# x copied into the result ahead of time, and the last product added to it by accumulating transfers from GpSimd

## What is computed

```python
xn = layernorm(x)
s  = attention(xn, ...)          # differential attention, RMS norm per head, then @ Wo
g  = silu(ffn(xn, ...))          # two layers of a mixture of 6 experts (top 2) with 2 shared ones;
                                 # each layer ends with y * rsqrt(mean(y*y) + eps) * norm_w[j]
return x + s * g
```

## Time and profile before

| | |
|---|---|
| median of 3 runs | 2025.4 us (2024.9 to 2025.41) |
| profiled execution, its own time | 2026.82 us |
| its span, first to last instruction | 2024.8 us |
| TensorE busy, share of the span | 93% |
| mean granted TensorE clock | 0.967 of full speed |
| layer two's blocks | about 1727 to 1946 us |
| last stage | about 1946 us to the end |

### The profile page before, as it was taken

The page is one execution under the profiler, slowest core; times in us unless marked ns, Lnnn a source line. Parts: engine busy times, 40 slices in busy tenths (PEclk is TensorE's granted clock), DMA queues, the critical chain, the costliest instruction groups (busy, mean ns, idle before and its releaser), DMA issues. The chain is left out here.

```text
span 2024.8 us, 42105 instructions
## 1 busy us (share of the span) xinstructions
PE 1881.6 (93%) x11851; PEld 1121.7 (55%) x11851; DVE 1466.7 (72%) x3474; ACT 1050.6 (52%) x2538; POOL 676.0 (33%) x728
## 2 busy tenths in 40 slices
PE   7888999999999999999999999999899999999975
PEld 4543334444343443434444347777788888787864
DVE  7888888888888898888888844444468855333348
ACT  3324667676676666667666644444333322344444
POOL 4542432111111232322323214777603432233334
PEclk9976999999999999999999999999999999999988
DMA  4443332212222121211212103343312112244363
GB/s 126 142 129 100 108 106 77 66 29 70 57 63 83 41 62 41 61 49 50 61 41 62 40 12 93 120 128 123 116 42 99 71 51 67 86 128 128 97 234 107
DMA packets 196441, 170.43 MB, mean 84 GB/s; under 512 B 92105, under 2 KB 176377, under 8 KB 195961
## 3 DMA queue, kind: packets, MB, share of 16 engines
q1 hardware_dynamic: 177288, 119.95, 20.7%
q0 software_dynamic: 15888, 46.16, 6.5%
q10 hardware_dynamic: 3168, 3.15, 0.5%
HBM read 104.16 MB, written 72.70 MB: 87 GB/s over the span
## 5 line engine op out<-in xcount | busy, mean ns | idle before, releaser
L1772 DVE TENSOR_REDUCE mx<-ps 128x1 f32<-128x512 f32 (+3 forms) x1536 | 762.2, 548 | 107.8 <-PE ps L904 84.7
L1363 ACT ACTIVATE fbuf<-ps 128x512 f32<-128x512 f32 (+3 forms) x1024 | 459.2, 508 | 253.9 <-PE ps L915 241.6
L900 PE MATMUL ps<-rbuf 72*128 72x512 bf16 (+3 forms) x1536 | 506.7, 337 | 33.0 <-DVE mx L1772 21.4
L915 PE MATMUL ps<-rbuf 75*128 75x512 bf16 (+3 forms) x1536 | 500.5, 333 | 18.0 <-DMA rbuf<-mrows 16.0
L915 PEld LDWEIGHTS ps<-rbuf 75*128 75x128 bf16 x1536 | 150.4, 98 | 326.1 <-ACT fbuf L1363 143.2
L1363 ACT ACTIVATE gbuf<-ps 128x512 f32<-128x512 f32 (+2 forms) x512 | 210.4, 470 | 106.3 <-PE ps L915 86.7
L749 POOL TENSOR_SCALAR_AFFINE_SELECT gbuf<-gbuf 128x512 f32<-128x512 f32 x96 | 61.3, 638 | 532.5 <-ACT gbuf L1363 532.5
L900 PEld LDWEIGHTS ps<-rbuf 72*128 72x128 bf16 x1536 | 152.0, 99 | 147.3 <-DVE mx L1772 101.2
L930 PE MATMUL ps<-fbuf 128*32 128x512 f32 (+3 forms) x2048 | 230.1, 522 | 3.1 <-ACT fbuf L1352 1.1
L904 PE MATMUL ps<-maskq,identb 128*128 128x128 bf16 x1024 | 230.3, 225 | 0.0
L756 POOL DMA_INDIRECT y_scr<-wstage,bidx x138 | 137.8, 998 | 248.1 <-ACT wstage L1407 222.2
(11 more groups left out here) (273 smaller groups left out, 2990.8 us busy)
## 6 DMA issues: line engine op xcount, KB each, us to landing
rbuf<-q_scr SPq DMA_DIRECT2D x192, 96.0 KB
xs_scr<-in_pad SPq DMA_DIRECT2D x8, 1360.0 KB, 6.2
gbuf<-xs_scr SPq DMA_DIRECT2D x69, 136.0 KB
gbuf<-xe_scr SPq DMA_DIRECT2D x69, 136.0 KB
rbuf<-k_scr SPq DMA_DIRECT2D x192, 48.0 KB
gbuf<-y_scr SPq DMA_DIRECT2D x8, 1024.0 KB
q_scr<-gbuf SPq DMA_DIRECT2D x48, 128.0 KB
gbuf<-a_scr SPq DMA_DIRECT2D x12, 512.0 KB, 5.0
```

What stands on the lines that cost most here:

```text
L900: ins = pe.matmul(o, qst[par][0:PROWS, i // 4, m, P * (i % 4):P * (i % 4 + 1)], kst[par][0:PROWS, m % 2, 512 * piece:512 * piece + width], ...
L915: pe.matmul(o, kst[par][0:SROWS, m % 2, P * j:P * (j + 1)], qst[par][0:SROWS, h, m, t0:C], start=True, stop=True).then_inc(b_scores, 1)
L1363: act.activation(prob(s)[:, t0:C], ps[:, s % SRING, t0:C], ACT.Exp, scale=SCALE).then_inc(b_exp, 1)
L1772: dve.tensor_reduce(mx[:, i // 4, piece, n:n + 1], ps[:, SRING + s % SRING, 0:width], AX, ALU.max, negate=True).then_inc(b_maxed, 1)
```

## The change

x no longer passes through SBUF in the last stage. Eight transfers of 512 KB from DRAM to DRAM copy x into the result; SP issues them after the row loads of blocks q = 10, 14, ..., 38. The product `gT` is then added to the result in DRAM by a transfer issued by GpSimd (`accum_op=ALU.add`), one for each chunk, the last one too. weigh(c) now waits until the transfer of chunk c - 2 has landed. GpSimd's additions, VectorE's last addition, the eight loads of x and SP's stores are gone. SP waits for all copies before it waits for the scatters of y and reloads it.

```diff
-            def load_x(c):
-                sp.dma_start(xres[c], xr[c]).then_inc(d_xearly if c < XEARLY else d_xlate, 16)
+            def copy_x(c):
+                sp.dma_start(ov[c], xr[c]).then_inc(d_xcopied, 16)
...
                 if odd == 0 and 0 <= i < NCH:
                     load_attn(i)
-                elif odd == 0 and NCH <= i < NCH + XEARLY:
-                    load_x(i - NCH)
-
-            sp.wait_ge(e_turned, TURNS)
-            sp.wait_ge(e_idx, TURNS)
-            load_x(3)
-            sp.wait_ge(e_u, TURNS)
-            load_x(4)
-            sp.wait_ge(e_down, TURNS)
-            load_x(5)
+                elif odd == 2 and 0 <= i < NCH:
+                    copy_x(i)
+
+            sp.wait_ge(d_xcopied, 16 * NCH)
             sent(1)
             for c in range(YSLOTS):
                 load_last_y(c)
-            load_x(6)
-            sp.wait_ge(d_turned, 3)
-            load_x(7)
             for c in range(YSLOTS, NCH):
                 load_last_y(c)
-            for c in range(NCH):
-                if c < NCH - 1:
-                    sp.wait_ge(d_fin, c + 1)
-                else:
-                    sp.wait_ge(d_sg, NCH + 1)
-                sp.dma_start(ov[c], xw[:, TB * c:TB * (c + 1), 0:E]).then_inc(d_out[c % 2], 16)
...
             def finish(c):
+
+                pool.wait_ge(d_xcopied, 16 * NCH)
                 pool.wait_ge(d_sg, c + 1)
-                if c < XEARLY:
-                    pool.wait_ge(d_xearly, 16 * XEARLY)
-                else:
-                    pool.wait_ge(d_xlate, 16 * (NCH - XEARLY))
-                pool.tensor_tensor(xw[:, TB * c:TB * (c + 1), 0:E], gT[:, c % 2].rearrange("p (k n) -> p k n", k=TB),
-                                   xres[c], ALU.add).then_inc(d_fin, 1)
+                pool.dma_start(ov[c], gT[:, c % 2].rearrange("p (k n) -> p k n", k=TB), accum_op=ALU.add
+                               ).then_inc(d_out[c % 2], 16)
 
             for c in range(NCH):
                 inv_rms(NCH + c)
                 if c > 0:
                     finish(c - 1)
+            finish(NCH - 1)
...
                 if c < 2:
                     dve.wait_ge(d_turned, c + 1)
                 else:
-                    dve.wait_ge(d_fin, c - 1)
+                    dve.wait_ge(d_out[c % 2], 16 * (c // 2))
...
-            dve.wait_ge(d_sg, NCH)
-            dve.wait_ge(d_xlate, 16 * (NCH - XEARLY))
-            dve.tensor_tensor(xw[:, NB - TB:NB, 0:E], gT[:, (NCH - 1) % 2].rearrange("p (k n) -> p k n", k=TB),
-                              xres[NCH - 1], ALU.add).then_inc(d_sg, 1)
```

More of the change, by code:

```diff
@@ L231, in build @@
         ain = [quarter(buf, i) for buf in (gbuf, rbuf[:, :].bitcast(F32)) for i in range(4)]
-        xres = [quarter(fbuf, 1), quarter(fbuf, 2), quarter(fbuf, 4), quarter(gbuf, 4), quarter(wqk, 0), quarter(fbuf, 3),
-                quarter(wstage[:, :, :].rearrange("p a n -> p (a n)"), 0), quarter(gbuf, 2)]
-        XEARLY = 3
         ytile = []
@@ L314, in build @@
         d_out = [sem(f"d_out{h}") for h in range(2)]
-        d_ain, d_xearly, d_xlate = sem("d_ain"), sem("d_xearly"), sem("d_xlate")
+        d_ain, d_xcopied = sem("d_ain"), sem("d_xcopied")
         d_yin = [sem(f"d_yin{s}") for s in range(YSLOTS)]
-        d_turned, d_aT, d_proj, d_nw, d_g, d_sg, d_fin = (
-            sem("d_turned"), sem("d_aT"), sem("d_proj"), sem("d_nw"), sem("d_g"), sem("d_sg"), sem("d_fin"))
+        d_turned, d_aT, d_proj, d_nw, d_g, d_sg = (
+            sem("d_turned"), sem("d_aT"), sem("d_proj"), sem("d_nw"), sem("d_g"), sem("d_sg"))
         block = ctx.enter_context(nc.Block())
@@ L804, in _ @@
                 send_out(1, q)
+            ov = out.rearrange("b (h k p) e -> (b h) p k e", h=2, p=P)
             def finish(c):
+                pool.wait_ge(d_xcopied, 16 * NCH)
                 pool.wait_ge(d_sg, c + 1)
-                if c < XEARLY:
-                    pool.wait_ge(d_xearly, 16 * XEARLY)
-                else:
-                    pool.wait_ge(d_xlate, 16 * (NCH - XEARLY))
-                pool.tensor_tensor(xw[:, TB * c:TB * (c + 1), 0:E], gT[:, c % 2].rearrange("p (k n) -> p k n", k=TB),
-                                   xres[c], ALU.add).then_inc(d_fin, 1)
+                pool.dma_start(ov[c], gT[:, c % 2].rearrange("p (k n) -> p k n", k=TB), accum_op=ALU.add
+                               ).then_inc(d_out[c % 2], 16)
             for c in range(NCH):
```

## The result

The changed kernel took 2038.48 us in the median of 8 runs, the kernel before 2024.67 us in the median of its 8. The ratio is 1.0076, with a 95% interval of 1.0059 to 1.0092: 0.8% slower, some 15 us. The forecast was 2031 us, slower, in a range of 2014 to 2048 us.

What follows compares the result with a forecast made beforehand. Bound: TensorE for most, VectorE in the last stage, slowed 2.1 us a turn by GpSimd's add. Copies +2.5, scatter -2.0, company +2.5, loop +2.2, last gate -1.2, end +1.7 = +5.7 us on 2025.4: 2031 us, range 2014 to 2048 us.

Steps and rivals of the forecast that it cites:

- L: Time from apply's end to its adding transfer's landing, taken as 5.75 us; the change's total is about 7 L - 34.6 us.
- the company: Last stage: the first adding transfer shares the DMA engines with the reload of y, +2.5 us (0 to +5).
- the late loads: Among the last four scatters: load_x(3) to (5) are gone, so the last scatter lands sooner, -2.0 us (0 to -2.5).
- the end: After apply(7): the last transfer's landing replaces VectorE's add of x and SP's store, +1.7 us (-0.6 to +3.9).
- the copies: Second layer's blocks: eight copies of x on SP's queue between row loads, +2.5 us (+1 to +7).
- the rival in which the addition was innocent: Last stage: GpSimd's add isn't what slows combine, VectorE's turn stays at 7.79 us; about +3 us, chance 0.04.
- The loop: Six turns from apply(0) to apply(6): each 8.15 us instead of 7.79 us, +2.2 us.
- Between apply(6) and apply(7): Last turn: squares and power are done early, so apply(7) ends 1.95 us after apply(6), not 3.15 us; -1.2 us.
- The quick: Last stage rival: the adding transfer lands in under 4.4 us; at 4.2 us the whole is -6 us; chance 0.20.
- the middling transfer: Last stage rival: the adding transfer lands in 4.4 to 5.5 us, no tellable change, 2021 to 2029 us; chance 0.18.
- the crowding copies: Blocks rival: copies hold up row loads at 1.08 us each, +7.1 us instead of +2.5 us, 2036 us; chance 0.08.
- The slow one: Last stage rival: adding serialises reading and writing row by row, landing in 8 us, +21 us, 2047 us; chance 0.18.

Runs made afterwards that it cites:

- e5: The kernel before, with GpSimd's seven additions of x moved to VectorE behind each apply; no copies, no adding transfers: 2013.95 us, ratio 0.9952.
- e10: The four-tile kernel of e1 with a GpSimd addition of gT to itself put ahead of each adding transfer: 2016.15 us, run once.
- e2: The changed kernel with GpSimd's transfers writing the product without adding, x left out of the result: 2020.31 us, run once.
- e1: The changed kernel with gT in four tiles instead of two, so weigh(c) waits for transfer c-4: 2013.81 us, ratio to before 0.996.
- e9: The changed kernel with gT in three tiles instead of two: 2011.75 us, ratio to before 0.9946.
- e7: The changed kernel with the reload of y left out for chunks 4 to 7: 2034.45 us, run once.
- e6: The four-tile kernel of e1 with the last chunk finished as before, VectorE adding x and SP storing: 2011.62 us, ratio to before 0.9941.
- e4: The kernel before with eight DRAM to DRAM copies of x into a scratch tensor added, its own loads of x kept: ratio 1.0005.
- e8: The changed kernel with the three late 512 KB loads of x put back, their data not used: 2039.02 us, run once.
- e3: The changed kernel with SP storing the product without adding, x left out of the result: 2017.59 us, run once.

## Why the prediction was right, point by point

The direction and the mechanism were as forecast: GpSimd's addition gone, VectorE's combines at 3.4 us, and in their place a wait of weigh for the landing. The size, +5.7 us against about +15 us by the ratio and +16.2 us in the traces, was too small, because L was mis-sized. The prediction names this as its own sign of failing: L outside 5.5 to 6.8 us. The direction held because L lies above the 4.9 us at which the forecast's line, 7 L - 34.6 us, is zero. With the measured L of 7.0 us that line gives +14.4 us. That it comes so close is in part luck, since the other misses nearly cancel: the company (+2.1 us), the late loads (+1.0 us) and the end (+0.8 us beyond the line) against the copies (-2.0 us).

- *What bounds the stage.* Right, and shown from both sides: e5 takes the addition away from GpSimd and the combines drop to 3.37 us; e10 puts one back and they rise to 5.01 us. This also removes the rival in which the addition was innocent.
- *L, 5.75 us.* This is the term that failed. The sum without the adding came out right, 0.1 + 2.05 + 1.45 + 0.7 = 4.3 us, where e2 measures 4.4 us on the mean. Its terms did not: the hand-over took 0.6 to 0.9 us, not 0.1 us, and from the start of the instruction to the landing it was mostly 3.4 us, where these terms give 4.2 us. The two errors cancel, which is luck. For reading the old values I took another pass at the full rate, 1.45 us. This is the step that failed: adding costs 2.6 us, by half the rate, a slow first microsecond, a tail, and 0.5 us more of descriptors. 7.0 - 5.75 = 1.25 us too little, paid seven times, are 8.8 us. The estimate of 4.4 us from the Trainium skill's two pages was lower still; the plain transfer of e2 takes as long.
- *The loop, +2.2 us.* Measured with the first turn's company set apart: 9.39 us a turn, 1.6 us over 7.79 us, times six, +9.6 us. e1 and e9 show that it is the wait: with three or four tiles, and no wait, a turn is 5.7 to 5.8 us, the 5.8 us that were worked out for VectorE alone.
- *The first transfer's company, +2.5 us.* Right in kind, too small: 14.01 - 9.39 = 4.6 us in the trace, 4.8 us by e7. It is the upper bound of 5 us.
- *Between apply(6) and apply(7), -1.2 us.* Measured -1.2 us.
- *The end, +1.7 us.* Measured +3.7 us. From the end of apply(7) to the landing it was 8.5 us, not 5.75 us, and the 4.5 us of closing, which I took as fixed, were 3.8 us. The last transfer is slower than the others (7.8 us from its start): apply(7) follows apply(6) by 1.93 us only, and transfer 6 started 1.7 us late, so the two start 0.95 us apart and share the engines. GB/s in 40 slices of 2020 to 2036 us has them in one stretch, the last byte at about 2031.6 us, 8.3 us after the end of apply(7):

```profile
GB/s 0 0 0 0 0 0 20 0 0 0 0 0 36 49 136 159 189 197 195 202 182 179 164 195 195 205 197 131 13 0 0 0 0 0 0 0 0 0 0 0
```

  I had the gain of one step (-1.2 us) feed a loss in the next and didn't see it. e6, with SP storing the last chunk, lands 1.9 us sooner.
- *The copies, +2.5 us.* Too large as far as the traces show. The stretch grew by 0.5 us here and by 1.6 us in e4, and neither can be told from nothing. I had charged the delays among the row loads to the 512 KB transfers between them; the quiet stretch had them nearly as often, 3.111 us a block against 3.175 us, and the lower bound, 0.25 us each, is nearer to what was measured.
- *The late loads, -2.0 us.* 4.37 to 2.40 us at the scatter, as forecast, and e8 shows the cause. Half of it reached VectorE: apply(0) came only 1.0 us sooner, since the first y took 5.82 us from its issue to the first combine, against 4.95 us before. Why y came in later isn't settled.
- *The rivals.* The quick and the middling transfer fell with L = 7.0 us, the crowding copies with e4. The slow one was the near miss: L lies between the forecast's 5.5 to 6.8 us and its 8.0 us. The quick case was also summed loosely: at L = 4.2 us the line gives -5.2 us, not -6 us.

## What to carry to other kernels

Before a step is handed to a transfer, ask who waits for it to land, and how many buffers are between them. The same adding transfers make this kernel 0.8% slower with two tiles and 0.4 to 0.5% faster than before with three or four. With two tiles only a combine of 3.4 us covers the 7 us from the end of apply to the landing; one more tile covers 5.7 us more. A term that no trace has, like L here, deserves a run of its own before the forecast when it is paid seven times. And when a helper engine's work blocks the engine that sets the pace (2.1 us a turn for an addition of 1.2 us), doing that work on the pacing engine itself can be the faster and smaller edit: e5 is 0.5% faster, and 5 of its some 10 us are traced to the turns.

## What the runs showed of the hardware

- An accumulating transfer of 512 KB from SBUF into DRAM, issued by GpSimd, with the engines to itself, lands 5.8 to 6.4 us after its instruction starts; without adding it is mostly 3.4 us, and SP's store 2.9 us. Its rate settles at 197 GB/s, against 328 to 377 GB/s, after a first microsecond at 45 to 119 GB/s. Its descriptors take 1.34 us instead of 0.82 us.
- A transfer that GpSimd waited to issue starts 0.6 to 0.9 us after its releaser ended in these traces (1984.11 to 1984.82 us), and 1.7 us for the seventh transfer of the changed kernel, while a GpSimd addition in the same place started after 0.08 us (1974.14 us by apply's end, 1974.22 us). Right behind GpSimd's own addition, in e10, the transfer starts at once: 1986.12 us, with the addition's end at 1986.17 us.
- With some 2 MB of the reload of y still to come (an estimate: 4 to 6 us of it at 388 GB/s), a plain store behind it on SP's queue lands after 11.3 us instead of 2.9 us (e3), a plain transfer beside it from GpSimd after 7.0 us instead of 3.4 us (e2), and an adding one from GpSimd after 10.8 us instead of 6.3 us. In these traces GpSimd's own queue was the sooner for the plain write, though e2's was issued 1.6 us later in the reload than e3's.
- A VectorE instruction with two inputs in SBUF, blocked by a GpSimd addition, waits most of that addition's time: 2.1 of 2.5 to 2.65 us, and 1.64 of 2.01 us in e10. The Trainium skill's rule ("SBUF — State Buffer", Who interferes with whom) names the pair; both traces agree with it. GpSimd's 1.3 us of descriptors beside the same combines (e1) cost VectorE nothing, 3.38 us each.
